# A graph network in one kernel: record scatters placed and paced anew, softmax and weighing joined in one block

## The reference

```
L0: h = mean of x[dst] over the edges of each src node; relu(h W1' + b1) W2' + b2
L1: q, k, v = x Wq.., e = edge_attr We (4 heads of 32)
    alpha = q[dst] . (k[src] + e) / sqrt(32)
    alpha = softmax of alpha over the edges that share dst
    agg   = segment_sum((v[src] + e) * alpha, dst)
    out   = agg + x Wskip + bskip;  out + gelu(gelu(out W1 + b1) W2 + b2)
L2: (x + 3 * segment_sum(weight * x[dst], src)) / 4
L3: per edge a product with the matrix of its type (9 types, both directions), summed by dst and by src
```

## Time and profile before

| | |
|---|---|
| timed runs | 4649.19, 4655.66, 4657.07 us; median 4655.66 us |
| span of the profiled execution | 4651.0 us |
| mean granted TensorE clock over the span | 0.754 |
| GpSimd busy | 3414.1 us (73%) |
| TensorE, VectorE, ScalarE busy | 2871.3, 2230.8, 613.9 us |
| scatters (L721) | 782, 1123.9 us, mean 1437 ns, 128.4 to 2635.7 us |
| blocks by their first instructions | link 143.9, l0 785, m0 948.7, project 1003, scores 1037, maxima 2062, weigh 2196.5, second 2400.7, norm 2568.6, gathers 2644.8 us |

### The profile page before, as it was taken

How to read it: one execution, slowest core, us unless ns; L and a number is a source line. 1 busy time by engine, 2 the same in 40 slices (tenths; PEclk the granted TensorE clock), 3 DMA queues, 4 the chain that set the end, 5 groups by cost and what they waited for, 6 DMA issues and landing times. The chain is left out here.

```text
span 4651.0 us, 50018 instructions
## 1 busy us (share of the span) xinstructions
PE 2871.3 (62%) x13750; PEld 2210.0 (48%) x13751; DVE 2230.8 (48%) x2711; ACT 613.9 (13%) x1076; POOL 3414.1 (73%) x3213
## 2 busy tenths in 40 slices
PE   3799998967777777751989643444444333333333
PEld 1688887943333333331989433333333333333333
DVE  7899997656666666668971621111111111111112
ACT  0355554010000000001751000000000000000000
POOL 1888886857777777767867677777777777777775
PEclk8899999968877878875999866666666566555556
DMA  6466566816666666651989523222222122212221
GB/s 191 139 189 183 170 187 209 265 37 172 170 170 170 170 171 173 173 153 59 278 241 276 174 68 94 68 68 68 68 68 68 49 53 52 53 53 53 53 53 51
DMA packets 498663, 599.91 MB, mean 129 GB/s; under 512 B 190115, under 2 KB 367441, under 8 KB 496248
## 3 DMA queue, kind: packets, MB, share of 16 engines
q0 software_dynamic: 117856, 246.12, 19.4%
q1 hardware_dynamic: 337751, 229.77, 17.7%
q10 hardware_dynamic: 42944, 122.68, 7.3%
HBM read 406.69 MB, written 204.36 MB: 131 GB/s over the span
## 5 line engine op out<-in xcount | busy, mean ns | idle before, releaser
L1151 PE MATMUL ps<-got,g_hot 128*128 x3224 | 719.2, 414 | 1151.3 <-DMA got<-y_back,s_msg 597.5
L721 POOL DMA_INDIRECT rec_by_src<-rec,pos x782 | 1123.9, 1437 | 344.1 <-issue 245.8
L1151 PEld LDWEIGHTS ps<-got,g_hot 128*128 128x128 f32 x3224 | 667.8, 316 | 1213.1 <-issue 1213.1
L1612 POOL DMA_INDIRECT sc_kv<-kv,d_src x806 | 762.0, 945 | 254.9 <-issue 245.3
L1036 POOL DMA_INDIRECT got<-y_forward,d_msg x782 | 739.1, 945 | 238.2 <-issue 238.2
L1036 POOL DMA_INDIRECT got<-y_back,s_msg x766 | 722.7, 943 | 241.7 <-issue 233.1
L806 PE MATMUL ps<-ln_low,ln_hot 128*125 128x256 f32 x2848 | 618.9, 380 | 19.7 <-DVE ln_low L783 15.9
L806 PEld LDWEIGHTS ps<-ln_low,ln_hot 128*125 128x125 f32 x2848 | 535.3, 188 | 103.2 <-issue 22.7
L1059 DVE TENSOR_TENSOR g_hot<-ps,src_loc 128x1024 f32<-128x1024 f32 x101 | 123.4, 1224 | 832.1 <-PE ps L1151 831.7
L1715 PE MATMUL ps<-q,sc_hotT 128*128 x1616 | 274.2, 322 | 236.4 <-DVE sc_hotT L1657 207.4
L1067 DVE TENSOR_TENSOR g_y<-ps,ms_b 128x384 f32<-128x384 f32 x75 | 41.8, 558 | 732.1 <-PE ps L1164 732.1
(11 more groups left out here) (328 smaller groups left out, 3102.4 us busy)
## 6 DMA issues: line engine op xcount, KB each, us to landing
linked<-ln_out SPq DMA_DIRECT2D x320, 224.0 KB
ve<-sc_kve ACTq DMA_DIRECT2D x202, 256.0 KB
wv_ve<-ve SPq DMA_DIRECT2D x101, 512.0 KB, 5.0
l_links<-linked SPq DMA_DIRECT2D x25, 800.0 KB, 7.3
l_links<-linked ACTq DMA_DIRECT2D x25, 800.0 KB, 9.2
attr_pairs<-ln_feats POOLq DMA_DIRECT2D x7, 2048.0 KB
sc_attr<-attr_pairs SPq DMA_DIRECT2D x202, 64.0 KB, 2.6
sc_kv<-kv,d_src POOLq DMA_INDIRECT x806, 3.0
```

Of the source, the lines that this page charges most:

```text
L721: pool.indirect_dma_start(out=dram["rec_by_src"], out_offset=bass.IndirectOffsetOnAxis(ap=S["pos"][:, c:c + 1], axis=0), in_=S["rec"][:, c ...
L1151: last = pe.matmul(ps[:, bass.ds(columns[j], width)], hot[:, q, j, :], got[:, bass.ds(slots[j], width)], start=False, stop=True, skip_grou ...
L1612: pool.indirect_dma_start(out=kv[:, q, j, :], out_offset=None, in_=dram["kv"], in_offset=bass.IndirectOffsetOnAxis(ap=S["d_src"][:, c:c + ...
```

## The change

(a) The number of scatters of each stage changes. (b) In index, 10 of them stand ahead of the wait for `tiled` and 14 behind the gathers. (c) In m0, project, second and norm the scatters wait for marks of progress: semaphores that the stage counts anyway, or, in second, a new one (`eased`) which four of the 25 products of each block increment. (d) The softmax and the weighing become one block. The four lists node, before, after and place are loaded in scores; v + e of the first six groups is fetched ahead of the shares; three groups are marked ahead. (e) The share is no longer exp(s) / sum but exp(s - ln(sum + 1e-16)): add, reciprocal and product become Ln and Exp on ScalarE and a subtraction on VectorE. (f) The transposes back use three PSUM banks (4 to 6), since banks 0 to 3 are cleared for the sums meanwhile. (g) The faces of ScalarE are made in `hot` itself, without the side buffer `away`. The multiplication with the shares (L1976) is as before.

```diff
-RECORD_PARTS = {"index": 6, "link": 302, "l0": 70, "m0": 30, "project": 22, "maxima": 82, "weigh": 100, "m1": 42, "l2": 76, "norm": 0}
+RECORD_PARTS = {"index": 24, "link": 312, "l0": 70, "m0": 25, "project": 15, "maxima": 88, "weigh": 106, "second": 104, "norm": 0}
...
+            if send is not None:
+                first, last = part_of(send)
+                send_some(pool, S, dram, first, last - LATER)
             for k, s in enumerate(stairs):
                 pool.wait_ge(tiled, k + 1)
                 pool.nop(nofuse=True)
@@ -469,10 +475,12 @@
                     pool.indirect_dma_start(out=s.rows[:, c, :], out_offset=None, in_=whole,
                                             in_offset=bass.IndirectOffsetOnAxis(ap=s.tile_i[:, c:c + 1], axis=0)).then_inc(got[k], 16)
             if send is not None:
-                send_records(pool, S, dram, send)
+                send_some(pool, S, dram, last - LATER, last)
 
         @block.sync
         def _(sp):
+            sp.wait_ge(fronted, 1)
+            sp.dma_start(dram["node"][0:1].rearrange("(a n) -> a n", a=1), front[:, :]).then_inc(begun, 16)
...
+            sp.wait_ge(begun, 16)
...
-            send_records(pool, S, dram, tag)
+            sent, last_sent = part_of(tag)
+            each = -(-(last_sent - sent) // CHUNKS)
+            for c in range(CHUNKS):
+                for sem, some in ((turned, each - 2 * (each // 3)), (hidden, each // 3), (product, each // 3)):
+                    pool.wait_ge(sem, c + 1)
+                    pool.nop(nofuse=True)
+                    send_some(pool, S, dram, sent, min(sent + some, last_sent))
+                    sent = min(sent + some, last_sent)
...
-            send_records(pool, S, dram, "m1")
-            send_records(pool, S, dram, "l2")
+            first, last = part_of("second")
+            free = last - first - BLOCKS * EASE
+            send_some(pool, S, dram, first, first + free)
+            for n in range(BLOCKS * EASE):
+                pool.wait_ge(eased, n + 1)
+                pool.nop(nofuse=True)
+                send_some(pool, S, dram, first + free + n, first + free + n + 1)
...
+                    if k in EASE_AT:
+                        last.then_inc(eased, 1)
...
-            send_records(pool, S, dram, "project")
+            first, last = part_of("project")
+            for n in range(last - first):
+                pool.wait_ge(product, max(1, n * BLOCKS // (last - first)))
+                pool.nop(nofuse=True)
+                send_some(pool, S, dram, first + n, first + n + 1)
...
+                if n == 4 * WAYS:
+                    for name, a in (("before", dram["node"][0:rows]), ("node", dram["node"][1:1 + rows]), ("after", dram["node"][2:2 + rows]),
+                                    ("place", dram["loc"].rearrange("b e -> (b e)")[0:rows])):
+                        sp.dma_start(S["mx_" + name][:, :], a.rearrange("(p c) -> p c", p=P)).then_inc(S["noded"], 16)
...
-                if n >= 4:
-                    pe.wait_ge(done, n - 3)
-                pe.transpose(ps[:, (n % 4) * BANK:(n % 4) * BANK + P], turn[:, n, :], S["ident"][:, :]).then_inc(turned, 1)
+                if n >= 3:
+                    pe.wait_ge(done, n - 2)
+                pe.transpose(turned_back(n), turn[:, n, :], S["ident"][:, :]).then_inc(turned, 1)
...
+            pe.wait_ge(cleared, 2)
...
+            send_records(pool, S, dram, "weigh")
...
-                act.activation(score[:, h, :], score[:, h, :], ACT.Exp).then_inc(exped, 1)
+                act.activation(back[:, h, :], score[:, h, :], ACT.Exp).then_inc(exped, 1)
+            for h in range(HEADS):
+                act.wait_ge(tallied, h + 1)
+                act.activation(back[:, h, :], back[:, h, :], ACT.Ln, bias=guard[:, 0:1]).then_inc(logged, 1)
+            for h in range(HEADS):
+                act.wait_ge(weighted, h + 1)
+                act.activation(score[:, h, :], score[:, h, :], ACT.Exp).then_inc(shared, 1)
+
+            def face(n):
+                i, q = divmod(n, WAYS)
+                act.wait_ge(summed[q], i + 1)
+                for j in range(OWN, GROUP):
+                    c = n * GROUP + j
+                    last = act.activation(hot[:, q, j, :], S["col"][:, :], ACT.Abs, bias=S["dst_loc"][:, c:c + 1], scale=-1.0)
+                last.then_inc(apart, 1)
+                act.wait_ge(apart, n + 1)
+                act.activation(hot[:, q, OWN:GROUP, :], hot[:, q, OWN:GROUP, :], ACT.Relu, bias=S["ones"][:, 0:1], scale=-1.0).then_inc(faced[q], 1)
...
+                dve.engine_nop().then_inc(tallied, 1)
+            for h in range(HEADS):
+                dve.wait_ge(logged, h + 1)
+                dve.tensor_tensor(score[:, h, :], score[:, h, :], back[:, h, :], ALU.subtract).then_inc(weighted, 1)
+            dve.wait_ge(weighted, HEADS)
+            dve.wait_ge(turned, HR)
+            dve.wait_ge(kept, HR)
+            dve.memset(ps[:, 0:TURN_AT * BANK], 0.0).then_inc(cleared, 1)
             dve.tensor_copy(iota[:, :], S["col"][:, :]).then_inc(numbered, 1)
             dve.wait_ge(numbered, 1)
...
+            for q in range(FIRST):
+                mark(0, q)
+            dve.wait_ge(done, HR)
+            weigh(0, 0)
+            dve.memset(ps[:, TURN_AT * BANK:BLOCKS * D], 0.0).then_inc(cleared, 1)
+            for q in range(1, WAYS):
+                if q >= FIRST:
+                    mark(0, q)
+                weigh(0, q)
+            with dve.Fori(1, WHOLE) as i:
                 for q in range(WAYS):
-                    group(i, q)
+                    mark(i, q)
+                    weigh(i, q)
...
+            first, last = part_of("norm")
+            for n in range(last - first):
+                if n:
+                    pool.wait_ge(biased, n * BLOCKS * PIECES // (last - first))
+                    pool.nop(nofuse=True)
+                send_some(pool, S, dram, first + n, first + n + 1)
+            pool.wait_ge(S["sent"], 16 * TILES)
```

More of the change, by code:

```diff
@@ L533, in climb_of @@
                 dve.engine_nop().then_inc(stepped, 1)
+            dve.memset(front[:, :], -1.0).then_inc(fronted, 1)
             dve.wait_ge(spread, 1)
@@ L1744, in softmax_maxima @@
         turn = m.sb("mx_turn", [P, HR, P])
[L1745 to L1748, removed]
+        node, node_b, node_a, loc = (S["mx_" + name] for name in ("node", "before", "after", "place"))
         bad = m.sb("mx_bad", [P, L])
@@ L1752, in softmax_maxima @@
         back = m.sb("mx_back", [P, HEADS, L])
-        open_b, open_a, open_s = (m.sb("mx_open" + n, [P, L]) for n in ("before", "after", "same"))
+        open_b, open_a, open_s = node, m.sb("mx_openafter", [P, L]), loc
         ends = m.sb("mx_ends", [P, 2 * HEADS])
@@ L1789, in _, with group @@
                     pe.wait_ge(refilled[h], 16)
-                if n >= 4:
-                    pe.wait_ge(done, n - 3)
-                pe.transpose(ps[:, (n % 4) * BANK:(n % 4) * BANK + P], turn[:, n, :], S["ident"][:, :]).then_inc(turned, 1)
+                if n >= 3:
+                    pe.wait_ge(done, n - 2)
+                pe.transpose(turned_back(n), turn[:, n, :], S["ident"][:, :]).then_inc(turned, 1)
+            pe.wait_ge(cleared, 2)
+            def group(i, q):
+                columns = load_columns(nc, S, mybir.EngineType.PE, "dst", 1, start_of(i, q))
+                pe.wait_ge(heated[q], i + 1)
+                pe.wait_ge(faced[q], i + 1)
+                pe.wait_ge(weighed[q], i + 1)
+                for j in range(GROUP):
+                    last = pe.matmul(ps[:, bass.ds(columns[j], D)], hot[:, q, j, :], ve[:, q, j, :],
+                                     start=False, stop=True, skip_group_check=True)
+                last.then_inc(summed[q], 1)
+            with pe.Fori(0, WHOLE) as i:
+                for q in range(WAYS):
+                    group(i, q)
+            for q in range(REST):
+                group(WHOLE, q)
         @block.gpsimd
@@ L1834, in _ @@
                              dram["alpha"][h].rearrange("(c p) e -> p c e", p=P)).then_inc(refilled[h], 16)
+            for n in range(WAYS, GROUPS):
+                bring(n)
         @block.vector
@@ L1838, in _ @@
             link = Chain(dve, order)
-            dve.memset(front[:, :], -1.0).then_inc(fronted, 1)
-            dve.wait_ge(noded, 16 * 4)
+            dve.wait_ge(S["noded"], 16 * 4)
+            link(dve.memset(guard[:, :], 1e-16))
             link(dve.tensor_scalar(bad[:, :], loc[:, :], 0.0, None, ALU.is_lt))
@@ L2286, in gnn_kernel @@
             S["alpha"] = a.sb("alpha_cols", [P, HEADS, PAIR_COLS])
+            for name in ("before", "node", "after", "place"):
+                S["mx_" + name] = a.sb("mx_" + name, [P, PAIRS_PAD])
+            S["noded"] = a.sem("mx_noded")
             with ExitStack() as early:
```

139 lines of the change are left out of this document (49 added, 90 removed).

## The result

The changed kernel takes 4678.5 us (median; 4672.8 to 4683.0), the kernel before 4654.3 beside it: ratio 1.0054, 95% interval 1.0040 to 1.0069. The forecast was 4654, with 4636 to 4668 as its range: it is slower, by more than 0.2%, and outside the range.

What follows compares the result with a forecast made beforehand. Each block ends with its last engine: VectorE in softmax and weighing. Merged block -10, index +8, second +0.3, norm +0.4 sum to -1.3 on the 4651.0 span: 4649.7; timed medians lie 4.7 higher, so 4654, range 4636 to 4668.

Steps and rivals of the forecast that it cites:

- Nothing to win: m0, project, second, norm: 5, 7, 14 and 14 scatters go, but these blocks did not end with GpSimd, so no gain.
- +0.3: Second: pacing makes the last scatter wait for a late TensorE mark, costing 0.3 us.
- 0 to +1, taken as +0.4: Norm: last scatter starts after the 73rd of 75 additions, its landing awaited beside the last stores; 0.4 us later.
- my own signs of being wrong: VectorE ends the merged block, first weighing starts after 2180 (times of before), or link starts before 148.
- Index, +8: Index: 24 scatters instead of 6, fourteen behind the gathers, so scatters end at 149.6 and the block ends 8 us later.
- the second rival: Index costs nothing: something else sets its boundary, 8 us shrink to 2 or less, about 4647; chance 0.07.
- Merged block, -10: Softmax and weighing: 194 scatters end at about 2389, 24 us after VectorE; block ends 10 us earlier, bounds -6 to -13.
- The softmax chain, -22: Merged block: Ln, Exp and subtractions replace adds and reciprocals; about 10 us instead of 31.85, 22 us less.
- the first weighing at 2168: Merged block: the weighing begins at about 2168, with 67 scatters done by then.
- Scores, link, m0, project at nothing: Scores' four added loads cost nothing, link's ten more scatters (20 us) are hidden, m0 and project gain nothing.
- The slower one: Rival in index: eight added scatters behind the gathers at 2.64 + 0.30 us each, 13 us more, 4667 to 4668; chance 0.10.
- The scatters keep up: Rival in the merged block: weighing does not hold scatters, they end at 2310, VectorE's 2365 counts; -25, 4631; chance 0.13.

Runs made afterwards that it cites:

- experiment 4: Changed kernel, in second all scatters but one sent at once, that one behind the wait for TensorE's last mark: 4675.7 us.
- Experiments 1 to 5: Changed kernel, single edits: second unpaced 4668.9, norm unpaced 4671.2, second with a bare late wait 4676.5, with one late scatter 4675.7, without GpSimd's closing drain 4667.9 us.
- experiment 2: Changed kernel with norm's 38 scatters sent at once instead of paced by marks: 4671.2 us.
- 7: Changed kernel with index, link, l0, second, project, scores and norm opened without GpSimd's closing drain: 4654.0 us.
- 8: As 7, and the shares copied to PSUM for the weighing: 4631.3 us.
- 10: As 8, and index's 14 late scatters moved to second (10 in index, 118 in second): 4634.5 us.
- 11: Changed kernel with shares copied to PSUM, second and norm unpaced, index's late scatters moved to second, all drains kept: 4627.3 us, ratio 0.9949.
- 12: As 11, with the seven blocks of 7 opened without GpSimd's closing drain: 4623.1 us, ratio 0.9943.
- 9: Kernel before the change, with the seven blocks of 7 and maxima opened without GpSimd's closing drain: 4648.3 us, ratio 0.9997.
- experiment 6: Changed kernel with the shares copied to PSUM by VectorE, once for six groups, and read there by the weighing: 4653.3 us, ratio 1.0006.

## Why the prediction was wrong, step by step

*"Their blocks did not end with GpSimd: the wait behind norm's last scatter was 8.14 us ... Nothing to win"; pacing "+0.3" and "0 to +1, taken as +0.4".* This is the step that failed: 0.7 us forecast for second and norm, 16.8 measured (9.1 and 7.7). That the two blocks did not end with GpSimd was true of the kernel before; but I read the 8.14 us as slack and gave the end of a block that GpSimd ends last no price of its own. GpSimd needs most of that time itself. In the changed norm it takes 6.8 us behind its last scatter, VectorE having ended 1.35 us before that, so of the 8.14 some 1.3 us were free:

```profile
2638.54 3.05 DVE L2216 TENSOR_TENSOR ms_y<-ps,ms_b 128x384 f32<-128x384 f32 x6 [0.55 <-DMA y_forward<-ms_y]
```

(norm of before: VectorE's end at 2641.59, 4.9 us behind the last scatter, and the gathers at 2644.84.) I took the pacing's cost as the last scatter's own delay, and it was right in that (experiment 4 shows it start 0.4 us ahead of TensorE's end), but pacing had brought the drain behind it. Experiments 1 to 5 show it for second; for norm experiment 2 shows 6.0 of the 7.7 us, and how they divide between the drain and the landing, and the rest, stay open.

The same missing price is in the merged block. Of the 31.5 us between the forecast of -1.3 and the +30.2 of the profiles, second has 8.8, norm 7.3, the merged block 14.4 (6.4 of it the boundary), index 2.0, and the rest -1.0. None of my own signs of being wrong fired: GpSimd ended the merged block, the first weighing started at 2171.2 in the times of before, and link did not start before 148. They tested the stream of scatters and not what stands behind it.

*Index, +8.* The scatters ended at 149.83 where 149.6 was forecast. Its +10.0 has the drain behind them. The floor, the store of node (141.6), showed once the drain was off it: link starts 6.2 to 7.4 us behind that store's issue in runs 7, 8, 10, 11 and 12. Before, its 143.89 was 4.5 us behind the last scatter (139.42), about the 4.1 of the changed kernel, which accounts for the 2.3 us that the second rival had unexplained; without the drain (9) link began 0.8 us behind the landing of the store.

*Merged block, -10, measured +4.4.* The mechanism was right, VectorE ahead and the scatters behind; two sizes were not. The stream ends at 2405.14, in the times of before 2396.8 instead of 2389: 68 scatters had started when the weighing began (67 forecast), but it began 3 us later and let through 100, not 103. The transposes back took 8.4 us, all at a granted clock of 0.50 and with 1.5 us of waits for copies out of the three banks, where before they took 6.0 with the clock rising from 0.50 to 0.90. And the stream had one idle stretch of 5.8 us, listed as issue. Every trace but that of the kernel before has one in this place, of 5.3 to 7.7 us; the kernel before has its one in second (9.85 us, ahead of the scatter at 2556.89). Its cause is open. And the boundary behind GpSimd took 8.3 us, where I had taken it equal to the 1.9 to 2.6 us behind VectorE: +6.4. My bounds of -6 to -13 had no term for it. That the drain takes these 8.3 us is carried over from second and not measured here; the boundary behind the weighing of before, with the same clearing of semaphores, was 1.9 us when GpSimd had long been done.

*The softmax chain, -22, and the first weighing at 2168.* 21.9, and 2171.2 in those times; the chain behind the loads of the scores began at 2088.48, that is 2080.1, as forecast. VectorE's end came at 2370.4 instead of 2365; it didn't matter, as stated.

*Scores, link, m0, project at nothing.* They gave back 1.7 us in all.

*The rivals.* The slower one had its place in index and was wrong: of the fourteen late scatters two took 2.4 and 2.7 us, one 1.5 and the rest 0.96. The Trainium skill, "SBUF — State Buffer", Who interferes with whom, infers that a tensor_tensor should not stall the generation of descriptors. The runs disagree again: with the second operand in PSUM the period fell from 1.90 to 1.30. Which access of the scatter is held, no run shows. "The scatters keep up" (4631) is the kernel that experiment 6 made of it, and without the tails 8 gives 4631.3; the agreement is chance, since experiment 6 shortens the block by 22.4 us and not by the rival's 33.5, and index cost nothing in 8 (link at 143.91) where the rival had 8. The case that was missing is the one that came: a price at the end of a block that GpSimd ends last, 4.1 to 8.8 us here.

## What to carry to other kernels

An idle stretch behind an engine's last instruction in a block isn't slack until one has seen what the engine does there; compare it with the end of the other engines in several blocks, and take the gaps behind blocks which that engine ended last as the range of its price. Here they were 4.1 to 8.8 us, so one block's figure is not another's. Work without a deadline belongs at a block's front, not spread to its end: evenly paced background work ends last by construction, and what it costs there is not its last item alone but all that closes the engine. Where a background stream bounds a block, look at what slows its period before shortening the foreground.

## What the runs showed of the hardware

- Behind a block that GpSimd ended last, the next began 8.8 us later in second, after a hundred paced scatters and after a single one; with a bare wait, the last scatter 42 us back, it was still 7.7 us behind TensorE. It was 4.1 us in index and 8.3 in the merged block, and at most 5.7 in second of the kernel before, where 118 scatters were sent at once and TensorE ended last. What the drain does in that time, and why it differs, is open.
- With the drain left out, the barrier no longer waits for scatters that are handed over but not yet generated: five of index's started after link's 142.24.
- A stream of scatters has one idle stretch that no other engine ends: 5.3 to 7.7 us in the merged block or the weighing in thirteen traces, 9.85 us in second in the kernel before. The cause is open.
- One operand of VectorE's 128x1024 multiplication moved from SBUF to PSUM took a scatter's period from 1.90 to 1.30 us.
